# One more level of VectorE sums ahead of the softmax denominators, and ones products of 256 columns

## The reference

```python
q = (layer_norm(x) @ Wq)          # heads of 64
k, v = split(layer_norm(ctx) @ Wkv)
k = apply_rope(k, cos, sin)
attn = clip(q @ k.T * 64 ** -0.5, -11, 11)
attn = softmax(attn, axis=-1)     # over the 1024 context rows
x = x + (attn @ v) @ Wo + bo
x = x + sum over 16 experts of sigmoid(h @ sel) * relu(h @ keys) @ values    # h = layernorm(x)
```

## Time and profile before

| | us |
|---|---|
| median of 3 runs | 1039.74 (1039.69 to 1040.93) |
| profiled execution, its own time | 1040.09 |
| its span, first to last instruction | 1037.9 |
| PE busy, share of the span | 987.5, 95% |
| DVE busy, share of the span | 821.8, 79% |
| ACT busy, share of the span | 514.9, 50% |
| POOL busy, share of the span | 256.5, 25% |
| attention, start of the feed-forward block's matmuls | 840.31 |

### The profile page before, as it was taken

The page is one execution under the profiler, slowest core; times in us unless marked ns, Lnnn a source line. Parts: engine busy times, 40 slices in busy tenths (PEclk is TensorE's granted clock), DMA queues, the critical chain, the costliest instruction groups (busy, mean ns, idle before and its releaser), DMA issues. The chain is left out here.

```text
span 1037.9 us, 15273 instructions
## 1 busy us (share of the span) xinstructions
PE 987.5 (95%) x5336; PEld 605.9 (58%) x5336; DVE 821.8 (79%) x1239; ACT 514.9 (50%) x759; POOL 256.5 (25%) x241
## 2 busy tenths in 40 slices
PE   4599999999999999999999999999999889999998
PEld 3455555555555555555555555555555358888886
DVE  5499999888989999999999978998889876545422
ACT  5465555555555555655555555555555442222221
POOL 5442423211111111211111100321000135545442
PEclk9799999999999999999999999999999899999999
DMA  6344333332323232322222233222222471332321
GB/s 172 114 143 126 100 93 106 100 93 68 92 67 93 71 102 89 97 87 73 87 72 88 71 93 83 82 82 82 82 62 64 130 256 53 122 123 101 123 82 41
DMA packets 68952, 100.34 MB, mean 97 GB/s; under 512 B 21968, under 2 KB 44752, under 8 KB 66832
## 3 DMA queue, kind: packets, MB, share of 16 engines
q1 hardware_dynamic: 68880, 99.41, 31.7%
HBM read 70.01 MB, written 10.75 MB: 78 GB/s over the span
## 5 line engine op out<-in xcount | busy, mean ns | idle before, releaser
L1033 ACT ACTIVATE wide_a<-score_ps 128x1024 f32<-128x1024 f32 x256 | 249.2, 1029 | 149.1 <-PE score_ps L846 149.1
L1239 DVE TENSOR_SCALAR wide_a<-wide_a 128x1024 f32<-128x1024 f32 x256 | 181.5, 740 | 74.9 <-ACT wide_a L1033 74.8
L1248 DVE TENSOR_TENSOR p_sum<-wide_a 128x1024 f32<-128x1024 f32 x128 | 161.7, 1263 | 2.3
L859 PE MATMUL o_ps<-wide_a,values_a 128*64 128x512 f32 x512 | 124.0, 605 | 0.0
L859 PE MATMUL o_ps<-wide_a,v_sb 128*64 128x512 f32 x512 | 124.0, 605 | 0.0
L846 PE MATMUL score_ps<-q_hi,k_hi 64*128 64x512 f32 x512 | 115.6, 448 | 0.8 <-DVE k_lo L1218 0.8
L1781 DVE SCALAR_TENSOR_TENSOR act<-h_ps,wide_a 128x512 f32<-128x512 f32 x64 | 44.2, 690 | 90.0 <-PE h_ps L147 88.2
L846 PEld LDWEIGHTS score_ps<-q_hi,k_hi 64*128 64x128 f32 x512 | 48.4, 185 | 111.9 <-issue 99.6
L1552 POOL TENSOR_TENSOR act_lo<-act,act_hi 128x512 fp32r<-128x512 f32 x64 | 84.8, 1324 | 96.5 <-ACT act_hi L1698 96.5
L1698 ACT CAST act_hi<-act 128x512 fp32r<-128x512 f32 x64 | 39.7, 621 | 135.4 <-DVE act L1781 135.4
L846 PE MATMUL score_ps<-q_hi,k_lo 64*128 64x512 f32 x512 | 102.0, 394 | 0.0
(11 more groups left out here) (203 smaller groups left out, 2006.5 us busy)
## 6 DMA issues: line engine op xcount, KB each, us to landing
wide_a<-sel_dram SPq DMA_DIRECT2D x16, 1024.0 KB, 4.6
k_swap<-k SPq DMA_DIRECT2D x124, 128.0 KB, 2.3
w_hi<-packs_hi SPq DMA_DIRECT2D x26, 384.0 KB, 3.9
w_lo<-packs_lo SPq DMA_DIRECT2D x26, 384.0 KB, 4.4
den<-inv_dram SPq DMA_DIRECT2D x64, 128.0 KB, 2.9
ctx_raw<-ctx SPq DMA_DIRECT2D x24, 128.0 KB, 2.3
packs_hi<-w_hi SPq DMA_DIRECT2D x8, 384.0 KB, 3.3
packs_lo<-w_lo SPq DMA_DIRECT2D x8, 384.0 KB, 3.6
```

The lines of the kernel that those rows point to most:

```text
L859: mm = pe.matmul(o_ps[DH * h:DH * h + DH, :], v_sb[n // 2 % 2][:, at:at + DH], probs[s % RING][:, h, :], start=(s == 0), stop=(s == STEPS ...
L1033: act.activation(probs[s % RING][:], score_ps[s % 2][:], ACT.Exp, scale=DH ** -0.5).then_inc(exp_done, 1)
L1239: dve.tensor_scalar(probs[s % RING][:], probs[s % RING][:], CLIP_HI, CLIP_LO, ALU.min, ALU.max).then_inc(clipped, 1)
L1248: dve.tensor_tensor(p_sum[m][:], first, second, ALU.add).then_inc(summed_up, 1)
```

## The change

DVE adds, behind `sum_quad(n-1, 1)` and ahead of `sum_up(n, 0)`, `p_sum[1]` (the sum of the first four tiles) to `p_sum[3]` (the sum of the last four). The four ones products each take 256 columns of this one sum: e is now the half of the columns, not the half of the steps. ACT copies 256 columns, `den_rows` holds 8 numbers in each of 128 partitions, and the addition of its halves falls away.

```diff
-    sh.den_rows = sb("den_rows", [P, 2, NQ // DH])
+    sh.den_rows = sb("den_rows", [P, NQ // DH])
...
@@ turn_den (SP)
-            row = sh.den[at:at + 1, :].rearrange("a (p j) -> a p j", p=DH)
-            sp.dma_start(sh.den_rows[DH * h:DH * h + DH, e, :], row).then_inc(sh.den_turned, DMA)
+            row = sh.den[at:at + 1, 0:NQ // 2].rearrange("a (p j) -> a p j", p=QUAD)
+            sp.dma_start(sh.den_rows[at:at + QUAD, :], row).then_inc(sh.den_turned, DMA)
@@ invert_den (DVE)
-    dve.tensor_tensor(sh.inv_rows[:], sh.den_rows[:, 0, :], sh.den_rows[:, 1, :], ALU.add).then_inc(sh.den_added, 1)
-    wait(dve, sh.den_added, n + 1)
-    dve.reciprocal(sh.inv_rows[:], sh.inv_rows[:]).then_inc(sh.den_inv, 1)
+    dve.reciprocal(sh.inv_rows[:], sh.den_rows[:]).then_inc(sh.den_inv, 1)
@@ denominators (PE)
-                pe.wait_ge(quads_up, 2 * n + 2)
+                pe.wait_ge(all_up, n + 1)
...
-                        mm = pe.matmul(side_ps[at:at + QUAD, :], ones[:], p_sum[2 * e + 1][:, h, :],
-                                       start=True, stop=True)
+                        mm = pe.matmul(side_ps[at:at + QUAD, 0:NQ // 2], ones[:],
+                                       p_sum[3][:, h, e * (NQ // 2):(e + 1) * (NQ // 2)], start=True, stop=True)
@@ evac_o (ACT)
-                act.copy(den[:], side_ps[:]).then_inc(den_evac, 1)
+                act.copy(den[:, 0:NQ // 2], side_ps[:, 0:NQ // 2]).then_inc(den_evac, 1)
@@ DVE
             def sum_up(n, m):
...
-                if m % 2 == 1:
+                if m == 3:
                     wait(dve, den_ready, n)
...
+            def sum_all(n):
+
+                dve.wait_ge(quads_up, 2 * n + 2)
+                dve.tensor_tensor(p_sum[3][:], p_sum[1][:], p_sum[3][:], ALU.add).then_inc(all_up, 1)
...
                     if m == 0 and n > 0:
                         sum_quad(n - 1, 1)
+                        sum_all(n - 1)
                     sum_up(n, m)
...
             sum_quad(NPAIR - 1, 1)
+            sum_all(NPAIR - 1)
             split_o(dve, sh, NPAIR - 2, 0)
```

More of the change, by code:

```diff
@@ L121, in shared_state @@
     sh.den_turned = sem("den_turned")
-    sh.den_added = sem("den_added")
     sh.den_inv = sem("den_inv")
@@ L378, in attention_phase @@
         quads_up = sem("quads_up")
+        all_up = sem("all_up")
         pv_done = sem("pv_done")
```

## The result

The changed kernel takes **1063.88 us** (median of 4 runs, 1062.73 to 1066.33) against 1039.74 us; the ratio is 1.0231, 95% interval 1.0212 to 1.0250. It is slower by 24.1 us, and the forecast of 1059.8 us was 4 us too low. The profiled execution took 1062.73 us, its span 1060.5 us.

What follows compares the result with a forecast made beforehand. A serial loop of DVE, o_lo, ACT's copies, exponential and clip was taken to bound the kernel; 40.3 - 5.9 - 7.1 - 6.4 - 0.4 - 0.4 = +20.1 us gave 1059.8 us, range 1052 to 1069 us.

Steps and rivals of the forecast that it cites:

- What bounds: Attention loop: DVE, o_lo, two ACT copies, exponential and clip close a serial loop; DVE's 2.12 us idle is no slack.
- The forecast's test: Sixteen attention iterations: DVE's first wait 1.9 in place of 2.12 us, PE's waits some 20 in place of 1.9 us.
- The added sum: sum_all on DVE: 1.26 us more per head pair, 32 times, 40.3 us; bounds 1.13 and 1.26 us a sum.
- The row with the 0.13 us behind a semaphore: Trace of a DVE sum waiting for the sum just ahead: 1.26 us against 1.13 us between independent instructions.
- Sum of rows and copy: L175 removed from DVE, 0.19 us each, -5.9 us; ScalarE's copy of den narrowed, 0.23 us each, -7.1 us.
- The rival "PE sets the time": DVE's idle time is slack and the ones products are on the path: 13.8 us faster, 1026 us; chance 0.04.
- The products: Ones products on PE: 0.43 us shorter each time, 13.8 us in all, none on the path in steady iterations.
- What the late iterations give back: From 595 us on, longer DVE work fills 7.0 us of DVE's idling for PE: -6.4 us.
- lowest bound: 1.13 us a sum, all 7.0 us given back, 2 us for L175's single 2.35 us: +13.4 us, 1053 us.
- the end: Behind the last sum, PE can start projecting y sooner because the ones products are shorter: -0.4 us.
- the clock: Rival: PE's longer waits make the clock fall, 11 x 2 = 22 us more, 1082 us; chance 0.07.
- My sign for it: The clock rival would show as a granted clock under 1.00 in the stretch of the sixteen iterations.

Runs made afterwards that it cites:

- e1: The changed kernel without its new sum, the denominators made of the last four probability tiles alone: 1025.96 us, ratio 0.9860.
- e2: The kernel before with 31 more VectorE sums of the same size at the same place, whose result nobody reads: 1074.74 us, ratio 1.0334.
- e5: The changed kernel with o_lo of pair n-2 computed right behind the first two clips, ahead of the sum of four: 1049.38 us, ratio 1.0089.
- e6: The kernel before with o_lo of pair n-2 computed right behind the first two clips, ahead of the sum of four: 1038.45 us, ratio 0.9978.
- e7: The changed kernel with the ones products of pair n-1 moved behind the scores of steps 2 and 3 of pair n: 1065.03 us, ratio 1.0237.
- e8: The changed kernel with both moves, o_lo ahead of the sums and ones products behind the scores of steps 2 and 3: 1031.82 us, ratio 0.9917.
- e9: The kernel before with both moves, o_lo ahead of the sums and ones products behind the scores of steps 2 and 3: 1041.10 us, ratio 1.0004.
- e4: The changed kernel with four more ones products of 512 columns per pair, results overwritten, ahead of PE's wait for the new sum: 1066.05 us, ratio 1.0241.
- e3: The changed kernel with ScalarE copying all 512 columns of side_ps to den, of which only 256 are used: 1069.18 us, ratio 1.0269.

## Why the prediction was right, point by point

Steady iterations:

| | us an iteration | against before |
|---|---|---|
| before | 24.39 | |
| changed | 25.30 | +0.91 |
| e1, without the new sum | 23.97 | -0.42 |
| e2, idle sum on the kernel before | 25.65 | +1.27 |
| e5, change and early o_lo | 24.42 | +0.03 |
| e6, early o_lo alone | 24.29 | -0.10 |
| e7, change and late products | 25.25 | +0.86 |
| e8, change and both moves | 23.87 | -0.52 |
| e9, both moves alone | 24.27 | -0.12 |

The mechanism was right. That the time came so near is in part luck, for errors of opposite sign met in the sum, as the last two points show.

- **What bounds**: the loop of DVE, o_lo, two copies, exponential and clip was forecast and holds, by e2 and e7 above all. The forecast's test came out: DVE's first wait went from 2.12 to 1.92 us, PE's from 1.9 to 19.4 us in these iterations (some 20 had been forecast).
- **The added sum**: 1.26 us was forecast, 1.27 measured in e2. The row with the 0.13 us behind a semaphore was the right one (1.25 against 1.14 us). The Trainium skill's page "VectorE: DVE Perf Modes", section "The DRAIN you can't avoid", measured that a semaphore costs nothing extra in a chain of eight copies; the same section says that a next operation that is not held back starts earlier. For this pair of sums the trace shows a cost of 0.11 us, and so does not agree with the first and does agree with the second.
- **Sum of rows and copy**: 0.42 us together in e1, as forecast; the copy's step fell by 0.20 to 0.21 us where the row of another stage had given 0.23.
- **The rival "PE sets the time"** was rightly dismissed, by the waits. It had leaned on PE's 95% and on the Trainium skill, "Perfetto Trace Analysis", section "Identifying the Most-Contended Engine". For TensorE that section wants, in place of the matmul busy share, the share of the peak arithmetic rate and the busy share of the weight loads. The latter is 58% in the earlier trace rows, under DVE's 79%, so the section speaks for this rival less than the prediction made of it.
- **The products**: 0.43 us, off the path, as forecast (1.00 to 0.57 us), and on it in e8 against e9 with 0.40.
- **What the late iterations give back**: -6.4 us was forecast, 7.8 came. From the o_lo of iteration 22 to the last one stand ten new sums (12.6 us), ten sums of rows (-1.9) and ten copies (-2.3): 8.4 us more without any give-back. Measured is 0.6:

```profile
596.17:836.45 240.28, 231.71 (x1292) 126.20 (x1284) 209.37 (x265) 129.63 (x165) 20.41 (x9) 0.99 0.31 90
```

```profile
618.27:859.14 240.87, 226.09 (x1284) 125.54 (x1280) 216.54 (x266) 125.82 (x165) 20.97 (x9) 0.99 0.31 91
```

  DVE's idle time, length less busy time, went from 30.9 to 24.3 us, 6.6 less. 2.3 of these are the copies, so only some 4.3 us were given back by waits for PE. The rest of the 7.8 is DVE work that got shorter: the one sum of rows that had taken 2.35 us is gone, which the forecast had in its lowest bound alone, and the clips took 1.4 us less. e4 shows the other side of it: there PE has hardly any room.
- **Where the 2.5 us of the span come from** by which the profiled execution exceeds 1037.9 + 20.1. The sixteen iterations took 14.6 us more (forecast 13.4), the four ahead of them 4.0 (3.4), and the beginning up to the first o_lo 3.4 (1.7: two new sums, less one sum of rows, one copy and the 0.4 of the products). The late part took 0.6 (2.0) and the end 0.1 less (0.4 less). So 3.6 us were missing in the first three and 1.1 too many in the last two. Of the beginning 0.8 us are there before the first new sum: the sum of four just in front of it starts at 77.92 in place of 77.11 us, and between 77.20 and 78.97 in the nine experiments, though the programs do not differ up to there, so this is scatter between executions. Of the other 2.8 us about 2 are, by the estimate below, a term left out of the sum, the clock. I had it as a rival with a chance of 0.07, 11 falls and 2 us for each, 22 us. My sign for it, a clock under 1.00 in the sixteen iterations, came out at 0.99; but the falls were fewer and cheaper.

One of the falls, on PE of the changed kernel:

```profile
237.25 0.64 PE L870 MATMUL side_ps<-p_sum,ones 128*32 128x256 f32 x8 [1.93 <-DVE p_sum L1257]
...
238.16 0.39 PE L844 MATMUL score_ps<-q_hi,k_lo 64*128 64x512 f32 x2
238.39 0.54 PE L844 MATMUL score_ps<-q_lo,k_hi 64*128 64x512 f32 x2
238.72 0.63 PE L844 MATMUL score_ps<-q_hi,k_hi 64*128 64x512 f32 x2
239.15 0.63 PE L844 MATMUL score_ps<-q_hi,k_lo 64*128 64x512 f32 x2
```

```profile
238.50:243.50 5.00, 5.00 (x25) 3.73 (x22) 2.80 (x8) 3.29 (x5) 1.07 (x1) 0.66 0.09 26
```

The wait of 1.93 us is followed, 1.5 us later, by matmuls of 0.63 in place of 0.39 us at the lower clock. The iteration from 239.06 to 264.50 us was 25.44 us long, the next of its kind (290.08 to 315.04) 24.96: 0.5 us for a fall, because PE's room swallows the rest. Of the nine waits of 1.9 us or more ahead of 600 us four had such a sequel (at 80.44, 132.65, 237.25 and 541.70 us) and five had none. With four falls the clock accounts for about 2 us of the profiled execution, by an estimate from this 0.5 us. Whether it is also what spreads the four runs over 3.6 us is open, and so are the 1.2 us between the profiled execution and the median: only one run of each kernel has a trace.

## What to carry to other kernels

Before adding work to an engine with idle time, ask whether its idle time shrinks when work is put ahead of it. Here the wait that kept one length in every iteration (2.12 us) belonged to a serial chain through another engine, and that engine's instructions in it cost in full although it is busy for half of the time; waits whose length changed from one iteration to the next (1.04 to 1.71 us in e6, 1.2 to 2.2 in e9) were slack beside a busy PE. A saving on the engine that looks busiest was worth nothing while such a loop was longer; open the loop first, by letting the instruction that releases the other engine go ahead of those that don't, and look at once for the next longest loop through the same instructions.

## What the runs showed of the hardware that was not expected

Waits of PE of about 2 us were enough, in some cases, for the granted clock to fall to its lower level (0.66 on average from 238.5 to 243.5 us): after four of nine such waits ahead of 600 us in the changed kernel, and after eight of eleven waits of 1.8 to 2.2 us in e3. In e7 it fell after one of 1.33 us (at 193.32 us). In the kernel before only the one of 3.60 us had gone with a fall in attention. And an instruction on VectorE that waits for its predecessor's semaphore started 0.11 us later (1.25 against 1.14 us) than one that does not, for sums of 128x1024 f32: 0.04 us behind the predecessor's end in place of 0.09 us ahead of it.
